# Holding back half of a matmul stage, and adding a bias by transfers, in a fused recurrent and feed-forward kernel

## The reference

```
xn  = layernorm(x)
i, f, o, z = split(xn @ W + b)                 # W: 256 x 1024
i = 10*tanh((i + input_bias)/10);  f = -softplus(f);  o = sigmoid(o);  z = tanh(z)
scan over the 2048 steps:  m' = max(f+m, i);  c = e^(f+m-m')*c + e^(i-m')*z
                           n = e^(f+m-m')*n + e^(i-m');  h = o*c/(n+1e-6)
x   = x + h/rms(h)*scale
g   = layernorm(layernorm(x))*gamma + beta
y   = silu(g @ w1 + b1)                        # w1: 256 x 1024 = (fc1_q - 128)*scales
x   = x + layernorm(x) + 0.5*(y @ w2 + b2)     # w2: 1024 x 256 = (fc2_q - 128)*scales
```

## Time and profile before

| | us |
|---|---|
| median of 3 runs | 310.28 |
| lowest and highest | 309.25, 311.25 |
| the profiled execution | 311.77 |
| its span | 310.0 |
| PE, DVE, ACT, POOL busy in it | 294.7, 269.5, 229.7, 126.4 |

### The profile page before, as it was taken

How to read it: one execution, slowest core, us unless ns; L and a number is a source line. 1 busy time by engine, 2 the same in 40 slices (tenths; PEclk the granted TensorE clock), 3 DMA queues, 4 the chain that set the end, 5 groups by cost and what they waited for, 6 DMA issues and landing times.

```text
span 310.0 us, 4767 instructions
## 1 busy us (share of the span) xinstructions
PE 294.7 (95%) x1728; PEld 256.3 (83%) x1728; DVE 269.5 (87%) x487; ACT 229.7 (74%) x370; POOL 126.4 (41%) x131
## 2 busy tenths in 40 slices
PE   7999999979899899999999999999999799988996
PEld 5778789856897789988897889987898699868896
DVE  3998989999899999999999997999999987692741
ACT  2699987889879966899876978599866983921720
POOL 3043058300290529512970179012992198155000
PEclk9999999899999999999999999999999979999999
DMA  7980021060000030012000300020000011000201
GB/s 266 349 304 0 0 44 27 0 135 2 0 1 2 34 101 5 0 66 71 1 2 34 102 2 0 0 71 1 0 2 34 3 33 68 2 0 2 70 0 68
DMA packets 11127, 14.73 MB, mean 48 GB/s; under 512 B 720, under 2 KB 10208, under 8 KB 10848
## 3 DMA queue, kind: packets, MB, share of 16 engines
q1 hardware_dynamic: 10368, 12.07, 11.3%
q0 software_dynamic: 320, 1.58, 2.6%
q10 hardware_dynamic: 416, 0.79, 0.7%
HBM read 8.67 MB, written 4.19 MB: 42 GB/s over the span
## 4 chain that ended last, share of the span: by engine, by line
PE 39%; DVE 38%; issue 11%; ACT 5%; POOL 5%; DMA 2%; DVEq 0%; POOLq 0%; ACTq 0%
PE z_ps L236 5%; PE z_ps L237 4%; PE z_ps L238 4%; DVE y_lo L854 4%; PE mm_ps L236 4%; PE mm_ps L237 4%; PE mm_ps L238 4%; DVE rec L763 3%; DVE rec L756 3%; DVE rec L778 3%; DVE g L822 3%; DVE bn L835 3%; PE mm_ps L329 2%; PE mm_ps L322 2%; DVE rows L830 2%
## 5 line engine op out<-in xcount | busy, mean ns | idle before, releaser
L236 PE MATMUL z_ps<-w_hi,y_hi 128*128 128x256 f32 x248 | 71.8, 290 | 2.6 <-DVE rows L891 1.9
L237 PE MATMUL z_ps<-w_lo,y_hi 128*128 128x256 f32 x248 | 70.9, 286 | 0.0
L238 PE MATMUL z_ps<-w_hi,y_lo 128*128 128x256 f32 x248 | 70.8, 286 | 0.0
L573 ACT ACTIVATE y<-mm_ps,b_all,unit 128x512 f32<-128x512 f32 x54 | 41.6, 770 | 12.8 <-PE mm_ps L329 12.8
L236 PEld LDWEIGHTS z_ps<-w_hi,y_hi 128*128 128x128 f32 x248 | 47.6, 192 | 3.8 <-DVE rows L891 2.1
L237 PEld LDWEIGHTS z_ps<-w_lo,y_hi 128*128 128x128 f32 x248 | 47.6, 192 | 0.3
L238 PEld LDWEIGHTS z_ps<-w_hi,y_lo 128*128 128x128 f32 x248 | 47.6, 192 | 0.0
L322 PE MATMUL mm_ps<-gt_hi,w_hi 128*128 128x512 f32 x124 | 39.9, 403 | 1.6 <-ACT y L573 1.6
L854 DVE TENSOR_TENSOR y_lo<-y,y_hi 128x512 fp32r<-128x512 f32 x56 | 37.6, 687 | 4.0 <-ACT y_hi L576 3.7
L236 PE MATMUL mm_ps<-xt_hi,wg_hi 128*128 128x512 f32 x96 | 38.4, 400 | 1.1 <-ACT f_gate L505 1.1
L329 PE MATMUL mm_ps<-gt_lo,w_hi 128*128 128x512 f32 x124 | 38.8, 394 | 0.0
(11 more groups left out here) (179 smaller groups left out, 665.2 us busy)
## 6 DMA issues: line engine op xcount, KB each, us to landing
out<-rows SPq DMA_DIRECT2D x15, 256.0 KB, 2.1
rows<-x SPq DMA_DIRECT2D x7, 512.0 KB, 6.5
q<-fc_q SPq DMA_DIRECT2D x2, 1024.0 KB, 10.8
wg_raw<-fc_scales SPq DMA_DIRECT2D x1, 1024.0 KB, 7.1
w_lo<-q POOLq DMA_DIRECT2D x1, 1024.0 KB, 7.0
wg_raw<-w_gates SPq DMA_DIRECT2D x1, 512.0 KB, 5.7
wg_raw<-w_gates ACTq DMA_DIRECT2D x1, 512.0 KB, 6.0
w_lo<-q POOLq DMA_DIRECT2D x1, 512.0 KB, 4.6
```

The lines of the kernel that those rows point to most:

```text
L236: pe.matmul(dst, wh[w_at], ah[a_at], start=start, stop=False)
L237: pe.matmul(dst, wh[w_at], al[a_at], start=False, stop=False)
L238: return pe.matmul(dst, wl[w_at], ah[a_at], start=False, stop=stop)
L573: act.activation(y[:, j % YBUFS], fc1_bank(c, j), ACT.Silu, bias=b1_all[:, j:j + 1], scale=unit[:, j:j + 1]).then_inc(silu_done, 1)
```

## The change

- fc2 of chunks 5 and 6: the first tiles of both banks are still made side by side. Of the second tiles, n = 1 follows g_turned, and n = 3 is held back: for chunk 5 until six tiles of fc1(6) are made, for chunk 6 until fc1(7) is done. `h_turned(7)` moves behind five tiles of fc1(6).
- y of chunk 6 goes to places of its own: the high parts into wg_hi and wg_lo, the low parts into xt_hi, xt_lo and a new tile y_more.
- `base_bias` is gone. `base(c)` ends with a transfer from POOL that adds b2_bc, repeated four times, into rows, after waiting for its own four instructions; `final(c, u)` waits for its landing.
- ACT makes all copies of the high parts of y of chunks 6 and 7, and g_normalised(7).
- The order of DVE in the tail is changed.
- fc1's scales arrive as rows [16, 128] and are transposed by PE; DVE copies them into s1. The idle passes are cut in two groups of eight around that. share_bc is laid into y.

The core of the diff:

```
@@ fc2 @@
+            def fc2_block(c, n, k):
+                dst, rows_of = fc2_out(c, n), slice(n * P, n * P + P)
+                hi, lo = y_high_of(c, k)[:, rows_of], y_low_of(c, k)[:, rows_of]
+                pe.matmul(dst, hi, w2_hi[:, k], start=(k == 0), stop=False)
+                pe.matmul(dst, hi, w2_lo[:, k], start=False, stop=False)
+                return pe.matmul(dst, lo, w2_hi[:, k], start=False, stop=(k == KF - 1))
-            def fc2_both(c, half):
+            def fc2_both(c):
                 for k in range(KF):
                     for u in range(2):
-                        if half == 0 and k == 0:
+                        if k == 0:
                             pe.wait_ge(final_done, at(c - 1, 2, u + 1))
-                        if half == 0 and u == 0:
+                        if u == 0:
                             pe.wait_ge(y_lo_done, at(c, 8, k + 1))
...
+                        fc2_block(c, 2 * u, k)
@@ tensor, start @@
-            idle_passes(IDLE_PASSES)
+            idle_passes(IDLE_PASSES // 2)
             pe.wait_ge(ident_ready, 2)
+            pe.wait_ge(s1_in, 16)
+            pe.transpose(mm_ps[:, 0, 0:KD * KF], s1_rows[:], ident[0:KD * KF, 0:KD * KF]).then_inc(s1_turned, 1)
+            idle_passes(IDLE_PASSES // 2)
@@ tensor, tail @@
-            fc2_both(5, 0)
+            fc2_both(5)
             g_turned(6)
-            fc2_both(5, 1)
-            fc1(6, range(0, 2))
+            fc2(5, [1])
+            fc1(6, range(0, 5))
             h_turned(7)
-            fc1(6, range(2, KF))
-            fc2_both(6, 0)
+            fc1(6, range(5, 6))
+            fc2(5, [3])
+            fc1(6, range(6, KF))
+            fc2_both(6)
             g_turned(7)
-            fc2_both(6, 1)
+            fc2(6, [1])
             fc1(7, range(KF))
+            fc2(6, [3])
             fc2(7, range(TT))
@@ scalar, tail @@
             g_normalised(6)
+            g_high(6)
             act.preload_act_table_set("natural_log_exp_and_others")
             reciprocal(7)
-            g_high(6)
             act.preload_act_table_set("silu_and_others")
             silu(6, range(0, 2))
             square_sums(7)
-            silu(6, range(2, 6))
-            silu_alone(6, range(6, KF))
+            silu(6, range(2, KF))
+            g_normalised(7)
             g_high(7)
-            for j in range(0, KF, 2):
-                silu(7, range(j, j + 1))
-                silu_alone(7, range(j + 1, j + 2))
+            silu(7, range(KF))
@@ vector @@
-            def base_bias(c):
...
             def final(c, u):
                 b = c % XBUFS
                 dve.wait_ge(fc2_done, at(c, 2, u + 1))
-                dve.wait_ge(biased, c + 1)
+                dve.wait_ge(biased[c % 2], at(c // 2, 16, 16))
@@ vector, start @@
-            dve.wait_ge(s1_in, 16)
+            dve.wait_ge(s1_turned, 1)
+            dve.tensor_copy(s1[:].rearrange("p k j -> p (k j)"), mm_ps[:, 0, 0:KD * KF]).then_inc(s1_out, 1)
+            dve.wait_ge(s1_out, 1)
@@ vector, tail (base_bias is also gone from the loop) @@
             g_low(5)
-            base_bias(4)
             denominators(7, range(KD))
             final(4, 0)
             mean_square(6)
+            final(4, 1)
             divisor(7)
...
             ln2(6)
-            final(4, 1)
             y_low(5, range(5, KF))
             numerators(7)
             o_times_c(7)
+            g_low(6)
+            final(5, 0)
             newton(7)
             refined(7)
-            g_low(6)
             h(7)
-            base_bias(5)
-            final(5, 0)
-            final(5, 1)
             y_low(6, range(0, 2))
             mean_square(7)
-            y_low(6, range(2, 3))
             h_scaled(7)
             residual(7)
-            y_low(6, range(3, 4))
+            y_low(6, range(2, 4))
             ln2_sums(7)
-            y_low(6, range(4, 5))
             ln2(7)
-            y_low(6, range(5, 6))
-            for j in range(6, KF):
-                y_high(6, j)
-                y_low(6, range(j, j + 1))
-            base_bias(6)
+            final(5, 1)
+            y_low(6, range(4, KF))
             g_low(7)
             final(6, 0)
+            y_low(7, range(KF))
             final(6, 1)
-            base_bias(7)
-            for j in range(KF):
-                y_split_last(j)
             final(7, 0)
@@ gpsimd @@
                     pool.tensor_scalar(rows[:, b, n], rows[:, b, n], up2[:, n:n + 1], nr2[:, 0, n:n + 1],
                                        ALU.mult, ALU.add).then_inc(base_done, 1)
 
+                pool.wait_ge(base_done, at(c, 4, 4))
+                pool.wait_ge(b2_halved, 1)
+                pool.dma_start(rows[:, b], b2_bc[:].unsqueeze(1).to_broadcast([P, TT, D]), accum_op=ALU.add
+                               ).then_inc(biased[c % 2], 16)
+
-            pool.dma_start(s1[:], fc1_scale_cols).then_inc(s1_in, 16)
+            pool.dma_start(s1_rows[:], fc1_scales.rearrange("k (j c) -> (k j) c", c=P)).then_inc(s1_in, 16)
...
             ln2_root(7)
-            g_normalised(7)
             base(7)
```

More of the change, by code:

```diff
@@ L45, in exists, with layer @@
     return 0 <= c < CHUNKS
-def layer(nc, x, w_gates, cols, scale_row, fc1_q, fc1_scale_cols, fc2_q, fc2_scales, b2_row, out):
+def layer(nc, x, w_gates, cols, scale_row, fc1_q, fc1_scales, fc2_q, fc2_scales, b2_row, out):
     x_view = x.rearrange("s (c t p) d -> s c p t d", t=TT, p=P)
@@ L160, in xt, with y_high_of, y_low_of @@
             return [y_hi[:, 0:KD], y_lo[:, 0:KD]] if c == 1 else [xt_hi[:], xt_lo[:]]
+        def y_high_of(c, j):
+            if c != CHUNKS - 2:
+                return y_hi[:, j]
+            return (wg_hi if j < 4 else wg_lo)[:, j % 4 // 2, j % 2 * T:j % 2 * T + T]
+        def y_low_of(c, j):
+            if c != CHUNKS - 2:
+                return y_lo[:, j]
+            if j < 4:
+                return (xt_hi if j < 2 else xt_lo)[:, j % 2]
+            return y_more[:, j - 4]
         ident_ready, half_ready, zeros_ready = sem("ident_ready"), sem("half_ready"), sem("zeros_ready")
@@ L188, in layer @@
         ln2_stat, ln2_r, g_done = sem("ln2_stat"), sem("ln2_r"), sem("g_done")
-        base_r, base_done, biased = sem("base_r"), sem("base_done"), sem("biased")
+        base_r, base_done = sem("base_r"), sem("base_done")
+        biased = [sem(f"biased{u}") for u in range(2)]
         gt_ready, gt_hi_done, gt_lo_done = sem("gt_ready"), sem("gt_hi_done"), sem("gt_lo_done")
         fc1_done, silu_done = sem("fc1_done"), sem("silu_done")
-        y_hi_done, y_lo_done, y_hi_own = sem("y_hi_done"), sem("y_lo_done"), sem("y_hi_own")
+        y_hi_done, y_lo_done = sem("y_hi_done"), sem("y_lo_done")
         fc2_done, final_done = sem("fc2_done"), sem("final_done")
@@ L343, in fc2 @@
                             pe.wait_ge(y_lo_done, at(c, 8, k + 1))
[L344 to L345 removed]
+                        ins = fc2_block(c, n, k)
                     if n % 2 or (c == CHUNKS - 1 and n == 2):
                         ins.then_inc(fc2_done, 1)
[L349 removed]
+            def fc2_both(c):
                 for k in range(KF):
                     for u in range(2):
[L353 removed]
+                        if k == 0:
                             pe.wait_ge(final_done, at(c - 1, 2, u + 1))
[L355 removed]
+                        if u == 0:
                             pe.wait_ge(y_lo_done, at(c, 8, k + 1))
[L357 to L361 removed]
+                        fc2_block(c, 2 * u, k)
             def x_turned(c):
@@ L575, in silu @@
                     act.wait_ge(silu_done, at(c, 8, j + 1))
-                    act.activation(y_hi[:, j], y[:, j % YBUFS], ACT.Copy).then_inc(y_hi_done, 1)
+                    act.activation(y_high_of(c, j), y[:, j % YBUFS], ACT.Copy).then_inc(y_hi_done, 1)
             act.dma_start(rows[:, 0, 2:TT], x_view[0, 0, :, 2:TT]).then_inc(x_landed[0], 16)
@@ L938, in _ @@
             dve.wait_ge(share_out, 2)
-            dve.scalar_tensor_tensor(out=w1_hi[:, 0], in0=q1[:, 0], scalar=-ZERO_POINT, in1=share_bc[:],
+            dve.scalar_tensor_tensor(out=w1_hi[:, 0], in0=q1[:, 0], scalar=-ZERO_POINT, in1=share_bc,
                                      op0=ALU.add, op1=ALU.mult).then_inc(w1_scaled, 1)
@@ L1253 @@
         "fc1_q": np.asarray(L0_ffn_fc1_q),
-        "fc1_scale_cols": np.ascontiguousarray(np.stack([by_partition(v) for v in np.asarray(L0_ffn_fc1_scales)],
-                                                        axis=1)),
+        "fc1_scales": np.asarray(L0_ffn_fc1_scales),
         "fc2_q": np.asarray(L0_ffn_fc2_q),
```

34 lines of the change are left out of this document (6 added, 28 removed).

## The result

The changed kernel takes 317.69 us (median of 4 runs, 316.62 to 319.07); the kernel before, run beside it, 309.91 (309.25 to 311.25). The ratio is 1.0248, with a 95% interval of 1.0187 to 1.0309: the change costs 2.5%, some 7.8 us. Its profiled execution took 316.79 us. Executions more than 1.5% above the fastest of their kernel are left out of all medians and ratios: two of ten, at 317.38 and 317.48 us, of the second kernel of experiment 2.

What follows compares the result with a forecast made beforehand. TensorE, busy 294.7 of 310.0 us, bounds the kernel, so only its waits move the end. Tail +2.6, middle +0.6, start +0.8 and clock +0.9 gave +4.9 us, on the median 310.28: 315.2 us, range 308.0 to 321.0.

Steps and rivals of the forecast that it cites:

- my last step: Putting the +4.9 us on the median, 310.28, since before's profiled execution, 311.77, lay 1.5 above it: 315.2 us.
- the middle: Loop, chunk 2's b2 landing at 166.4 delays x_low(6): TensorE's 0.65 us wait becomes 1.25, +0.6 (-0.65 to +2.5).
- the start: Kernel's beginning: scales as rows, turned by TensorE, delay its first transposes by 0.9; +0.8 us counted (-0.9 to +2.4).
- the tail: Chunks 4 to 7: last matmul at 309.9 instead of 307.3, +2.6 us; its end is 299.1 + 2l.
- l: Time from base's last instruction to b2's landing: 5.4 us (3.3 to 7.3); the end of the kernel breaks even at 4.1.
- the half of an amount I had no row for: b2's transfer, four times as many pieces: a possible extra 1 us would give 5.9 to landing; the middle, 5.4, taken.
- The clock: Lower clock behind TensorE's new waits late in the kernel: 0.4 plus 0.5, together +0.9 us (bounds 0 and 2).
- the long wait: TensorE ahead of h_turned(7), 262.4 to 266.8: 4.4 us, as h(7) stands behind final(5, 0) and chunk 5's landing.
- the second wait: TensorE in fc2_both(6), waiting for final(5, 1) at 276.6: 2.1 us; half a chance of a clock step behind it.
- The fast transfer: Rival: b2's transfer lands in 3.3 us and the order wins, -3.3, 307.0 us; chance 0.15.
- the slow one: Rival: b2's transfer, held up by its pieces or DVE, takes 7.3 us, +10.6, 320.9 us; chance 0.20.
- Short waits: Rival: both TensorE waits real but short, landing near 4.2 us, no clock step, 311.4 us; chance 0.20.

Runs made afterwards that it cites:

- the second kernel of experiment 2: Changed kernel with final(5, 0) behind h(7) and rms_root(7) ahead of base(6) on GpSimd: 313.76 us, ratio 1.0115.
- experiment 1: Changed kernel with parts undone: bias by VectorE 310.14 us (1.0003), start of before 317.11 (1.0234), both 309.84 (0.9978); kernel before with only the transfers 315.60 (1.0170).
- experiment 3: Changed kernel with one edit in the loop, final(t - 3, 0) moved behind input_times_z, x_low and maximum: 313.79 us, ratio 1.0112.
- the first kernel of experiment 2: Changed kernel with only final(5, 0) moved from ahead of newton(7) to behind h(7): 317.19 us, ratio 1.0237.
- experiment 5: Changed kernel, transfers kept, start of before, each final moved so VectorE first does what TensorE needs: 305.85 us (0.9857); same order, bias by VectorE: 307.41 (0.9902).

## Why the prediction was right

The forecast was 315.2 us, in a range of 308 to 321, by +4.9 us on the profiled execution; the two profiled executions lie 5.0 apart (311.77, 316.79). By the medians the change costs 7.8 us, 2.9 more than forecast, and came out at 317.69, 2.5 above the forecast. 1.5 of that is my last step: I took before's profiled execution to lie 1.5 above its median for a reason that would hold for the changed kernel too. It does not: the changed kernel's profiled execution lies 0.9 below its median, which is the rest. Its four runs had mean clocks of 0.978 to 0.989, the slowest the lowest, though the two at 0.984 lie 2.0 us apart (316.62, 318.58). Only the profiled pair can be followed wait by wait, so what makes up the other 2.8 of the 7.8 us is not known.

That the sum met the pair's 5.0 to a tenth is in part luck: in that pair the middle was 1.2 to 1.3 too low, the start 0.8 and the tail 0.2 too high, and the errors nearly cancel.

| step | forecast | profile after |
|---|---|---|
| l, base's end to landing | 5.4 | 0.30 + 5.1 = 5.4 |
| wait in the middle | 1.25 (+0.6) | 2.58 (+1.9) |
| VectorE ahead of `final(4, 0)` | 2.9 | 3.11 |
| TensorE before g_turned(6) | 1.2 | 0.69 + 0.25 + 0.94 = 1.88 |
| h(7) ends | 266.8 | 268.25, or 266.5 less the 1.8 of the middle |
| TensorE before h_turned(7) | 4.4 | 3.83 |
| TensorE in fc2_both(6) | 2.1 | 2.02 |
| TensorE before g_turned(7) | 0 | 0 |
| tail | +2.6, clock +0.9 | +3.3 together |
| start | +0.8 | 0 against before at 101.8 us, 0.5 against the changed kernel with the start of before |

**What bounds it, and the mechanism**: right. TensorE's busy time did not change, and the end moved by its waits alone. The decisive term, a transfer that lands 5.4 us after the rescaling, was the 4.6 of the smaller accumulation, 0.3 ahead of it, and 0.5 for the smaller pieces, the half of an amount I had no row for. The landings measured 5.4 at the median and 5.5 where they held VectorE up, and so the wait at `h_turned(7)` came to within 0.6 us. Undoing the bias alone brings the ratio back to 1.000 (experiment 1): that is shown. What remains an argument is why 512 KB take 5.1 here and 4.6 in the earlier trace rows; the four times smaller pieces were my reason, and no run here has the same transfer in larger pieces.

**The middle** was mis-sized: +0.6 against +1.9. I kept base(2)'s end at 161.0, as it was the earlier trace rows. It ended at 162.12: it started 2.25 later and took 1.14 less. With that 1.1 and the 0.1 by which this landing was later than l, the middle would have been +1.8. GpSimd stands at the head of this chain, and its own position has to be forecast, not only what follows from it. It stayed within the bounds given (-0.65 and +2.5).

**The start** was mis-sized the other way, by 0.3 or more. The local delay came, and was larger than I took it to be (1.82 us at chunk 1, experiment 1), but most of it was made up for by 101 us, 0.4 of it in the wait there, where I had counted 0.6 for such a wait. What is left is 0.5 us at 101 us, 0.4 at the end, and 0.6 (start alone) and 0.3 (with the bias by VectorE) by the medians, none of it clear of the intervals.

**The clock.** The forecast was a step behind the long wait, most of it hidden by the next. In the profile:

```profile
258.00:264.00 6.00, 6.00 (x30) 4.99 (x29) 0.09 (x1) 5.87 (x7) 5.38 (x9) 1.00 0.55 87
264.00:270.00 6.00, 2.17 (x12) 1.73 (x10) 5.38 (x6) 0.75 (x4) 1.35 (x1) 0.80 0.67 131
270.00:272.00 2.00, 2.00 (x10) 1.68 (x9) 0.17 (x1) 1.95 (x8) 0.56 (x1) 0.74 0.00 0
```

The step is there, and the 2.02 us wait that follows hides it: TensorE would have been earlier at `fc2_both(6)` without it and waited longer, as the pair of experiment 3 shows, where 1.38 us more of low clock shortened this wait by 1.38. There was no step behind the second wait. With the tail at +3.3, the 2.6 + 0.9 of the forecast were 0.2 too much. What this hiding is worth I did not say: in the first kernel of experiment 2 the long wait is the last one, and its step cost 2.7 us.

**The rivals.** The fast transfer and the slow one both fall with the durations of the eight transfers, in the view of L1183:

```profile
DMA to landing us min/median/max: 5.1/5.1/5.8
```

The Trainium skill's fit (DMA: Bandwidth & Descriptors, Anatomy of one DMA — SWDGE (gpsimd) path), 3.2 us for this size by the estimate ahead, does not agree with the 5.1 measured; the measurement decides. The "DVE blocks DMA" trap of the Trainium skill (SBUF — State Buffer, SBUF: two separate sides) would have GpSimd's transfers start late while VectorE holds the ports that they share. No run here shows that: the median was 5.1 us in every kernel with these transfers, whichever way VectorE's order was; the longest single one took 5.3 to 6.7 us from issue to landing, and why those took longer is not known.

"Short waits" falls with the wait of 3.83 us at h(7). The point that decided between faster and slower, l = 4.1 for the tail, is l in *this* order: experiment 5 has the same l and gains 1.4%. This I did not say. The forecast named the cost of a landing as a property of the change, and it is one of where its waiter stands.

## What to carry to other kernels

Work moved from a busy engine to a DMA saves that engine's time only if the instruction that waits for the landing stands behind everything that the bounding engine needs next; otherwise each landing costs its full latency, minus what the engine had in hand (here a kernel at +2.3% or one at -1.4%, with the same eight transfers). When a wait is taken away, look for the next instruction in line on each engine before counting the gain: the wait at `h_turned(7)`, 3.83 us, removed by moving `final(5, 0)`, came back as 2.2 us more of waiting at the next bank and 2.7 of low clock behind it. A low clock behind a wait cost nothing here where a further wait outlasted it, and 2.7 us where none followed. A duration measured while the neighbouring engine stood still is not to be counted on once it works.
